# Five engines of one attention pipeline take their steps in a new order

## The reference

```python
def attention(q_in, keys, Wq, bq, Wk, bk, Wv, bv, Wo, bo):
    w = softmax((q_in @ Wq + bq) @ (keys @ Wk + bk).T / 16)
    return w @ (keys @ Wv + bv) @ Wo + bo

x1 = x + attention(x, ctx, *L0)
x2 = x1 + attention(ln(x1), ln(ctx), *L1a) + attention(ln(x1), ln(side), *L1v)   # ln with gains and biases
x3 = x2 + ln(x2) @ fc_W + fc_b
S = (x3 @ Wq2 + bq2) @ (ctx @ Wk2 + bk2).T / 16
x4 = x3 + softmax(S, axis=over_the_tokens_of_x3) @ (ctx @ Wv2 + bv2)
h = ln(x4) * gamma + beta
out = h + attention(h, ctx, *L3)
```

## Time and profile before

| what | value |
|---|---|
| median of the runs | 600.93 us |
| the profiled execution, its own time | 600.17 us |
| its span, first to last instruction | 598.1 us |
| mean granted clock of TensorE | 0.985 |
| busy: TensorE, VectorE, ScalarE, GpSimd | 574.3, 470.1, 444.9, 502.4 us |
| matmuls | 4712 |
| DMA bytes | 44.58 MB |

### The profile page before, as it was taken

One profiled execution on the slowest core, in us unless ns is written; L12 is line 12 of the kernel. 1 busy time (PEld: TensorE's weight loads), 2 busy tenths in 40 slices (PEclk: granted clock), 3 DMA queues, 4 the chain that ended last, 5 costly groups with the idle time before them and its releaser, 6 DMA issues.

```text
span 598.1 us, 16329 instructions
## 1 busy us (share of the span) xinstructions
PE 574.3 (96%) x4712; PEld 559.4 (94%) x4712; DVE 470.1 (79%) x1470; ACT 444.9 (74%) x1520; POOL 502.4 (84%) x700
## 2 busy tenths in 40 slices
PE   4699999999999999999999999999999999999994
...
PEclk9799999999999999999999999999999999999997
...
DMA packets 30375, 44.58 MB, mean 75 GB/s; under 512 B 2768, under 2 KB 22096, under 8 KB 30288
## 3 DMA queue, kind: packets, MB, share of 16 engines
...
## 4 chain that ended last, share of the span: by engine, by line
PE 87%; DVE 6%; issue 2%; ACT 1%; DMA 1%; SPq 1%; POOL 0%; DVEq 0%; ACTq 0%; POOLq 0%
PE bank L672 14%; PE bank L685 9%; PE bank L655 9%; PE bank L679 9%; PE bank L663 7%; PE bank L696 5%; PE bank L823 5%; PE bank L698 5%; PE bank L697 5%; PE bank L801 5%; PE bank L713 4%; PE bank L785 3%; PE bank L786 3%; PE bank L787 3%; PE bank L814 1%
## 5 line engine op out<-in xcount | busy, mean ns | idle before, releaser
L915 ACT ACTIVATE prob_L<-bank,neg_max_L 128x128 f32<-128x128 f32 x320 | 114.4, 378 | 18.5 <-DVE neg_max_L L1241 18.3
L1396 POOL TENSOR_TENSOR rstd_ln<-var_eps_ln,minus_half 128x2 f32<-128x2 f32 x64 | 45.1, 705 | 29.6 <-ACT var_eps_ln L925 29.3
L915 ACT ACTIVATION_READ_ACCUMULATOR prob_L<-bank,neg_max_L 128x1 f32 x320 | 69.4, 217 | 0.0
L1241 DVE TENSOR_REDUCE neg_max_L<-bank 128x2 f32<-128x256 f32 (+1 forms) x128 | 59.1, 476 | 11.7 <-PE bank L679 9.4
L1055 DVE TENSOR_TENSOR oT_lo_L<-bank,oT_hi_L 128x256 fp32r<-128x256 f32 (+1 forms) x96 | 48.2, 504 | 21.3 <-ACT oT_hi_L L868 20.3
L868 ACT ACTIVATE xT_hi_L<-bank 128x512 fp32r<-128x512 f32 (+1 forms) x96 | 58.4, 612 | 8.1 <-PE bank L655 5.8
L868 ACT ACTIVATE oT_hi_L<-bank 128x256 fp32r<-128x256 f32 (+1 forms) x96 | 44.9, 472 | 20.7 <-PE bank L685 19.2
L868 ACT ACTIVATE probT_L<-bank 128x256 f32<-128x256 f32 (+1 forms) x96 | 45.4, 473 | 9.0 <-PE bank L663 8.8
L1204 DVE BATCH_NORM_STATS2 stats_ln<-x 128x6 f32<-128x256 f32 x128 | 47.7, 414 | 0.9
L1055 DVE TENSOR_TENSOR xT_lo_L<-bank,xT_hi_L 128x512 fp32r<-128x512 f32 x64 | 43.6, 681 | 6.0 <-ACT xT_hi_L L868 5.3
L663 PE MATMUL bank<-ident,prob_L 128*128 128x128 f32 x256 | 43.7, 274 | 2.1 <-ACT prob_L L915 2.1
...
## 6 DMA issues: line engine op xcount, KB each, us to landing
...
```

The source lines that it names most:

```text
L915: last = activation(at(prob[k], g)[:, b, :], block(bank, b), ACT.Exp, bias=at(neg_max[k], g)[:, b:b + 1], accum_out=at(total[k], g)[:, b:b ...
L1241: dve.tensor_reduce(at(neg_max[k], g)[:], scores, AX.X, ALU.max, negate=True).then_inc(done[f"max_{k}"], 1)
L1396: pool.tensor_tensor(at(rstd[k], g)[:], at(var_eps[k], g)[:], minus_half[:, 0:n], ALU.pow).then_inc(done[f"rstd_{k}"], 1)
```

## The change

Only the numbers of STARTS and PREPARATIONS change. Every step, preparation, transfer and buffer stays. The diff, cut to three of the steps and parts of the preparations:

```diff
@@ -20,211 +20,211 @@
 STARTS = {
-    "load_x": [106, 274, 292, 1025, 2353, 2946, 4243, 5234, 5584, 6767, 8682, 10768, 12656, 14797, 16109, 17737, 19412, 21080,
-        23051, 24432, 26210, 27825, 28797, 31403, 34032, 34933, 37320, 38138, 39793, 41489, 43050, 43914],
-    "Q_L0": [895, 2397, 3429, 3817, 4747, 6222, 8239, 10343, 12117, 14166, 15589, 17350, 19041, 20684, 22413, 24030, 25787,
-        27476, 27954, 30935, 32398, 34590, 36089, 37758, 39401, 40977, 42664, 43230, 44394, 46359, 47591, 48550],
-    "OUT_L3": [11702, 12737, 14378, 14741, 16682, 18374, 20104, 21790, 23433, 25460, 26809, 28817, 30164, 31895, 34057, 35696,
-        37179, 38773, 39074, 42040, 43841, 45850, 47971, 50373, 52318, 54021, 55132, 55718, 56111, 56620, 56975, 57643],
...
+    "load_x": [196, 328, 334, 2547, 2798, 3132, 3703, 4610, 4972, 6708, 7280, 10034, 12298, 14044, 15060, 17178, 19024, 21981,
+        22107, 24220, 25258, 28150, 29545, 31438, 32769, 34238, 35298, 38765, 41549, 41871, 43100, 44925],
+    "Q_L0": [1765, 2793, 3295, 3724, 4518, 5037, 6882, 7637, 10035, 12920, 14558, 15848, 18534, 19453, 21268, 23278, 24315,
+        25980, 28641, 31100, 31508, 33380, 34660, 37480, 38769, 39858, 42127, 44025, 45190, 46076, 47601, 47972],
+    "OUT_L3": [9144, 12620, 12850, 15733, 16033, 18746, 20862, 22269, 23118, 23370, 23970, 27638, 30280, 30570, 32306, 33450,
+        34359, 41967, 42197, 42674, 42931, 43336, 46599, 47243, 53562, 54543, 55333, 56023, 56248, 56520, 56744, 56967],
...
 }
-PREPARATIONS = {"M_L0": 395, "N_L0": 528, "m_L0": 484, "n_L0": 615, "M_L1a": 1381, "N_L1a": 1614, "m_L1a": 1470, "M_L1v": 2081, "N_L1v":
-    2752, "m_L1v": 2170, "n_L1": 2223, "n_fc": 1527, "mean_fc": 1702, "M_L2": 1789, "k_L2": 1876, "M_L3": 3073, "N_L3": 3166,
-    "m_L3": 3253, "n_L3": 3342, "M_hi_L0": 504, "N_hi_L0": 635, "M_hi_L1a": 1490, "N_hi_L1a": 1738, "M_hi_L1v": 2190,
-    "N_hi_L1v": 2887, "gained_fc": 1525, "F_hi": 2260, "M_hi_L2": 1896, "Wv2_hi": 1707, "M0_L3": 3183, "M_hi_L3": 3209,
-    "N_hi_L3": 3273, "scaled": 396, "M_lo_L0": 545, "N_lo_L0": 677, "m_col_L0": 584, "bias_L0": 723, "wk_L1a": 1265, "wq_L1a":
-    870, "bvp_L1a": 1367, "wv_L1a": 1419, "M_lo_L1a": 1624, "N_lo_L1a": 2065, "m_col_L1a": 1663, "wk_L1v": 1522, "wq_L1v": 1670,
-    "bvp_L1v": 2098, "wv_L1v": 2626, "M_lo_L1v": 2249, "N_lo_L1v": 2929, "m_col_L1v": 2288, "bias_L1": 2434, "bias_fc": 2150,
-    "centred_fc": 2183, "F_lo": 2334, "M_lo_L2": 2295, "k_bias2": 2394, "Wv2_lo": 2401, "M_lo_L3": 3292, "N_lo_L3": 3344,
...
-    "rows_L3": 1821, "load_qk_L0": 70, "load_cols": 82, "load_vo_L0": 88, "load_rows_L0": 100, "load_qk_L1a": 112,
-    "load_rows_wq_L1a": 124, "load_rows_wkv_L1a": 136, "load_vo_L1a": 148, "load_qk_L1v": 160, "load_rows_wq_L1v": 172,
-    "load_rows_wkv_L1v": 184, "load_vo_L1v": 196, "load_rows_L1": 208, "load_fc": 220, "load_qk_L2": 232, "load_v_L2": 244,
-    "load_qk_L3": 554, "load_vo_L3": 729, "load_rows_L3": 256}
+PREPARATIONS = {"M_L0": 1491, "N_L0": 1383, "m_L0": 1579, "n_L0": 1224, "M_L1a": 2870, "N_L1a": 1093, "m_L1a": 2959, "M_L1v": 2354, "N_L1v":
+    2443, "m_L1v": 2310, "n_L1": 4589, "n_fc": 835, "mean_fc": 931, "M_L2": 508, "k_L2": 595, "M_L3": 3206, "N_L3": 3119,
+    "m_L3": 3635, "n_L3": 3459, "M_hi_L0": 1600, "N_hi_L0": 1490, "M_hi_L1a": 2979, "N_hi_L1a": 1292, "M_hi_L1v": 2508,
+    "N_hi_L1v": 2587, "gained_fc": 833, "F_hi": 1192, "M_hi_L2": 615, "Wv2_hi": 1161, "M0_L3": 3452, "M_hi_L3": 3321, "N_hi_L3":
+    3226, "scaled": 396, "M_lo_L0": 1651, "N_lo_L0": 1532, "m_col_L0": 1644, "bias_L0": 2355, "wk_L1a": 1755, "wq_L1a": 2428,
+    "bvp_L1a": 893, "wv_L1a": 978, "M_lo_L1a": 3022, "N_lo_L1a": 1354, "m_col_L1a": 3061, "wk_L1v": 1251, "wq_L1v": 1858,
+    "bvp_L1v": 3823, "wv_L1v": 2253, "M_lo_L1v": 3409, "N_lo_L1v": 2824, "m_col_L1v": 2388, "bias_L1": 4798, "bias_fc": 944,
+    "centred_fc": 1080, "F_lo": 1387, "M_lo_L2": 704, "k_bias2": 743, "Wv2_lo": 1207, "M_lo_L3": 3573, "N_lo_L3": 3875,
...
+    2185, "load_qk_L0": 208, "load_cols": 88, "load_vo_L0": 172, "load_rows_L0": 310, "load_qk_L2": 94, "load_qk_L1a": 226,
+    "load_rows_wq_L1a": 268, "load_rows_wkv_L1a": 112, "load_v_L2": 184, "load_vo_L1a": 124, "load_qk_L1v": 160,
+    "load_rows_wq_L1v": 244, "load_rows_wkv_L1v": 148, "load_vo_L1v": 256, "load_rows_L1": 70, "load_fc": 136, "load_qk_L3":
+    1650, "load_vo_L3": 1496, "load_rows_L3": 286}
```

More of the change, by code:

```diff
@@ L22 @@
 STARTS = {
-    "load_x": [106, 274, 292, 1025, 2353, 2946, 4243, 5234, 5584, 6767, 8682, 10768, 12656, 14797, 16109, 17737, 19412, 21080,
[5 rows of a table removed]
-    "load_ctx": [280, 298, 310, 322, 328, 334, 340, 346, 352, 358, 11007, 11992, 13812, 14148, 16208, 17898, 19448, 21276,
[3 rows of a table removed]
-    "hi_ctx": [2035, 2312, 2762, 3030, 4092, 4320, 5871, 7846, 9665, 11494, 13440, 15196, 16796, 18634, 20287, 21961, 23546,
[5 rows of a table removed]
-    "lo_ctx": [2092, 2635, 3170, 4031, 4932, 5710, 7903, 9691, 11409, 13247, 15132, 16769, 18376, 20072, 21741, 23517, 25225,
-        26746, 28547, 28873, 31916, 34018, 35568, 37431, 38772, 40328, 41955, 43702, 44802, 45699, 47662, 48917],
@@ new lines @@
+    "hi_ctx": [578, 1380, 1562, 1787, 2079, 2331, 2727, 5113, 9728, 11326, 12782, 16117, 16594, 18560, 21293, 22563, 22641,
[5 rows of a table added]
+    "lo_ctx": [629, 1516, 1790, 2086, 2335, 2784, 5652, 9823, 11423, 12882, 16070, 16692, 18636, 21484, 22162, 22729, 24008,
+        25730, 28680, 31178, 32451, 32755, 33924, 37046, 37690, 39492, 42485, 43694, 44644, 45723, 48889, 50272],
+    "load_side": [82, 316, 322, 1185, 3383, 4092, 5879, 7043, 8014, 8868, 9669, 11934, 13919, 15790, 16706, 18163, 20767, 23512,
[5 rows of a table added]
+    "x_bias": [2407, 2533, 2856, 3368, 4470, 4686, 6568, 6693, 9895, 12158, 13904, 14557, 17038, 18148, 21842, 21967, 23498,
+        25118, 28010, 29155, 31052, 32629, 33284, 33799, 34635, 41401, 41731, 41857, 44785, 46116, 46242, 48569],
@@ new lines @@
+    "stats_keys": [578, 2897, 3448, 3691, 4034, 4392, 6305, 7464, 8304, 9147, 10382, 13052, 14169, 16369, 17170, 18711, 21163,
+        23777, 24832, 26515, 28362, 30298, 30875, 34105, 35210, 36812, 38025, 41326, 41606, 43689, 43814, 47138],
+    "rstd_keys": [885, 3118, 3778, 4078, 4302, 6184, 7041, 8458, 8866, 9724, 12059, 14030, 15902, 16764, 18274, 20821, 23692,
[15 rows of a table added]
+    "norm_keys": [1031, 3228, 3938, 5725, 6889, 7860, 8714, 9515, 11780, 13765, 15636, 16552, 18008, 20612, 23358, 24401, 26103,
[11 rows of a table added]
@@ new lines @@
+    "stats_lnf": [5730, 7361, 7941, 9477, 10118, 11627, 14059, 16690, 17396, 18380, 20275, 24318, 24695, 26306, 27300, 29436,
+        30772, 34360, 35457, 37330, 37674, 38288, 40814, 43346, 44032, 47264, 48098, 49182, 51157, 52420, 53329, 54347],
+    "rstd_lnf": [5990, 7685, 8263, 9655, 10421, 11920, 14254, 16863, 17584, 18567, 20544, 24541, 25050, 26700, 27564, 29656,
+        30983, 34511, 36014, 37552, 37956, 38457, 40998, 43520, 44254, 47467, 48286, 49337, 51608, 52616, 53511, 54545],
+    "lo_fc": [5971, 7763, 8184, 10222, 10626, 13178, 14652, 16554, 17692, 18575, 20445, 23939, 25571, 26640, 27808, 29742,
+        30627, 34619, 35560, 37511, 37854, 39639, 41215, 43286, 44909, 47900, 49051, 51080, 51535, 52824, 53554, 54500],
```

38 lines of the change are left out of this document (13 added, 25 removed), and 310 rows, old and new, of tables (PREPARATIONS, STARTS).

## The result

The changed kernel takes 604.23 us (median, 603.54 to 604.46), and the kernel before 600.82 beside it: 1.0055 times as long, 95% interval 1.0038 to 1.0073. The forecast was 596.5, faster, with a range up to 603. It was wrong in sign, and the time lies outside its range.

A forecast was written before the change was run, and what follows sets the result against it. TensorE, busy for 96% of the span, was taken to bound the kernel; from the profiled 600.17 us, start -4.1, stretch +3.6 and tail -3.7 gave 595.9, with 0.76 added 596.5 us, range 589.5 to 603.

The forecast's parts named there:

- The start: Up to Q_L1 of group 0: work needing no wq goes first, Q_L1(0) at 46.6 instead of 50.72, gain 4.1 us.
- wk_L1a done at 21.9: VectorE in the start: weights complete near 19.4, then GpSimd's product, four VectorE instructions and 0.7 us for handovers.
- The bound of 3 us late transfers: Lower bound of the start's gain: 1 us if first transfers come 3 us late.
- wq_L1a 4.65: VectorE in the start: wq_L1a priced like a whole wq in the earlier trace, 4.65 us, ending at 33.1.
- From there to Q_L1(0) 13.5: VectorE from wq_L1a's end to lo_L1(0): 51 instructions, 13.5 us, to 46.6, with room on the other engines.
- A start over 49 refutes the walk: Sign in the start: Q_L1 of group 0 should stand near 46.6; over 49 the walk is refuted.
- The bounds of the term: Start's gain: 6.5 us with full-stretch VectorE rate and early transfers, 1 us with first transfers 3 us late.
- The second rival: New start: TensorE may stand at 22 to 33 us, the clock falls, costing about 4 us: 600.5; chance 0.09.
- no gap over 4 us: Sign in the start: no TensorE gap over 4 us behind the first matmul, clock 1.00 from about 12 us.
- The stretch: 60 to 560 us: steps placed close behind producers raise waits from 2.1 to 5.7 us, +3.6 us.
- The first and third rivals: Full stretch: first, no new waits, 593, chance 0.18; third, close places stall it, 12.6 us more, 605.5, chance 0.15.
- The tail: Last group's OUT_L2 to the end: 38 more matmuls fill idle time, 4.5 us less 0.8, gain 3.7 us.

The follow-up runs named there:

- new_bias_later: Changed kernel with GpSimd taking x_bias(0), x_bias(1) and x_bias(2) behind lo_L0(2) instead of ahead of it; 601.96 us, before 601.13: 1.0018.
- new_bias_apart: Changed kernel with x_bias(0) behind lo_L0(2) and x_bias(1), x_bias(2) behind norm_keys(1) on GpSimd; 601.12 us, before 600.90: 1.0000.
- two tests: TensorE steps taken one place back: 60 close behind producers in the changed kernel, 612.95 us; 17 seen waiting in new_bias_apart, 607.83 us.
- The joined kernels: Old order up to Q_L1(1) or OUT_L2(28), then new: 605.61, 603.07 us; new then old at these places: 610.03, 610.64; before 601.49.

## Why the prediction was wrong

**The start is the step that failed**, and in it the price of wq. Forecast against trace, each with what it adds to the delay of Q_L1(0):

- wk_L1a done at 21.9; measured 24.1: +2.2. The transfers as a whole ran as reckoned, but WkT_L1a needed 6.6 us from issue and landed at 21.8, where its place in the bytes had it at 19.4. Transfers don't land in the order of their issues: row_L1v_b, issued behind it at 16.40, landed ahead of it, at 21.2. The bound of 3 us late transfers covers this.
- wq_L1v 4.65; measured 5.6 (24.11 to 29.69): +0.9, here too beside GpSimd. Seven small instructions 1.8; measured 1.7: -0.1.
- wq_L1a 4.65; measured 8.0: **+3.4**. The 4.65 came from the earlier trace rows, where GpSimd is idle for more than half of the time, and was used for a place in which it has six long instructions in a row. The earlier trace rows had the warning in it: product_wq at 1.76 us where its like took 1.05 and takes 0.68 undisturbed. I took the duration and did not ask why the two differed. new_bias_later shows the cause.
- From there to Q_L1(0) 13.5; measured 15.5 (39.4 to 54.87): +2.0. TensorE was to have room beside the VectorE. It had none: from 39.89 to 54.87 it isn't idle once, and it works at the lower clock up to 46.1. The VectorE stands idle for 2.9 us in this time, in four waits of 0.5 to 1.1.

Together 8.3 us, up to rounding: 46.6 became 54.87. "A start over 49 refutes the walk" applied. The bounds of the term, a gain of 6.5 to 1 us, didn't hold it, since none of them asked for a *longer* instruction: a loss in the start was possible, and the bounds had left it out.

**The second rival**, the clock falling in the new start, happened, somewhat later than its place (between 22 and 33 forecast, 36 to 40 seen). The trace shows 3.52 us idle and the lower level from 39.3 to 46.1, over 6.2 us of work. By the rule of the Trainium skill named there such a gap puts the array back to half rate, and the trace agrees. Half of 6.2 is some 3 us, an estimate of what it cost; it is no second cause beside wq_L1a, since with wq_L1a at 4.63 us (new_bias_later) the gap at this place is 0.56 us and no fall follows it. It was given 0.09 because I had looked for gaps with steps at undisturbed lengths. The sign "no gap over 4 us" was met and told nothing: the clock fell by the end of a gap of 3.52 us here and of 2.52 us in new_bias_later, and it stayed at 1.00 over one of 2.16 us in new_bias_apart.

**The stretch** came out right in size: +3.4 for +3.6. Waits ended by a producer were 2.1 and are now 4.4 (waits of the weight loads, 60 to 560 us; the rows left out end by "issue"):
```profile
PEld bank L696 <- DVE oT_lo_L L1055: 1.4, 5, 0.5
PEld bank L655 <- DVE x L1268: 1.3, 4, 0.4
...
PEld bank L672 <- DVE xT_lo_L L1055: 0.8, 3, 0.3
PEld bank L785 <- DVE xT_lo_fc L1055: 0.5, 2, 0.3
...
PEld bank L655 <- DVE x L1274: 0.2, 1, 0.2
PEld bank L679 <- ACT qT_L L978: 0.2, 1, 0.2
```
L696, L785, L679 and L655 were forecast, the L672 was not; 4.4 is less than the 5.7 forecast for them. So these waits grew by 2.3 us where the whole 3.6 was put on them, and all rows of the view together, those ended by "issue" too, only from 4.4 to 5.7. The rest of the 3.4 is in no row, and the reason (closeness) found no support in two tests. The number was right in part by luck, and its reason is not shown. The first and third rivals (no new waits; 12.6 us more) are out.

**The tail** was right: -3.2 for -3.7, 17.2 us from OUT_L2 to the last matmul for 17.5, 104 matmuls for 102, TensorE busy 14.3 us where over 12 was asked. The joined kernels give the same gain whatever lies ahead of it.

The start alone accounts for the miss: 604.2 - 7.7 = 596.5. (The forecast's own sum is slightly off: 600.17 - 4.1 + 3.6 - 3.7 is 595.97, and with 0.76 it gives 596.7.) A range that ended at 603 had no room for a start that gets worse.
